# Cross-attention and gated feed-forward: V times the output weights once per head ahead of the rounds, one packed product per round, and the last feed-forward by tiles of 128 rows

## The reference

```python
# x (8, 256, 256), ctx (8, 77, 256); 16 heads of 64; hidden size 768; all fp32
xn   = layernorm(layernorm(x)) * gamma + beta
q    = (xn @ w_q).reshape(B, 256, 16, 64)
k, v = split(ctx @ w_kv)                       # (B, 77, 16, 64) each
attn = softmax(einsum('bqhd,bkhd->bhqk', q * 64 ** -0.5, k))
o    = einsum('bhqk,bkhd->bqhd', attn, v).reshape(B, 256, 1024)
x    = x + (o @ w_out + b_out) * tanh(gate)
y    = layernorm(x)                            # weights below are integers / 127
x    = x + (silu(y @ wg.T) * (y @ wu.T)) @ wd.T
```

## Time and profile before

| | us |
|---|---|
| three runs | 316.48, 316.53, 320.73 |
| median | 316.53 |
| the profiled execution | 315.11 |
| its span in the trace | 313.3 |
| granted TensorE clock, mean | 0.998 |
| T0 of rounds 0 to 7 starts at | 60.4, 90.0, 121.5, 151.0, 180.6, 210.1, 239.7, 269.1 |
| end of O1 of the last round | 293.3 |

### The profile page before, as it was taken

One profiled execution on the slowest core, in us unless ns is written; L12 is line 12 of the kernel. 1 busy time (PEld: TensorE's weight loads), 2 busy tenths in 40 slices (PEclk: granted clock), 3 DMA queues, 4 the chain that ended last, 5 costly groups with the idle time before them and its releaser, 6 DMA issues.

```text
span 313.3 us, 6353 instructions
## 1 busy us (share of the span) xinstructions
PE 295.8 (94%) x2371; PEld 272.2 (87%) x2371; DVE 231.6 (74%) x599; ACT 170.6 (54%) x325; POOL 165.7 (53%) x164
## 2 busy tenths in 40 slices
PE   6899999897987999999999999999999999999994
PEld 6898977686985999889988989898989899978984
DVE  2298887586785887878887787779787878785653
...
DMA packets 16314, 23.29 MB, mean 74 GB/s; under 512 B 1634, under 2 KB 13898, under 8 KB 16282
## 3 DMA queue, kind: packets, MB, share of 16 engines
...
HBM read 15.87 MB, written 4.62 MB: 65 GB/s over the span
## 4 chain that ended last, share of the span: by engine, by line
PE 77%; POOL 11%; DVE 3%; issue 3%; ACT 3%; DMA 2%; POOLq 0%; SPq 0%; DVEq 0%; ACTq 0%
PE ps L786 12%; PE ps L736 8%; PE ps L722 7%; PE ps L696 5%; PE ps L704 5%; PE ps L700 5%; PE ps L623 4%; PE ps L832 4%; PE ps L836 4%; PE ps L833 4%; PE ps L816 3%; PE ps L819 3%; POOL probs L1045 3%; POOL t_lo L1052 3%; PE ps L631 2%
## 5 line engine op out<-in xcount | busy, mean ns | idle before, releaser
L1045 POOL TENSOR_TENSOR probs<-probs,total 128x616 f32<-128x616 f32 x32 | 38.9, 1217 | 75.5 <-DVE total L1170 75.5
L917 ACT COPY pt<-ps 77x512 f32<-77x512 f32 x64 | 34.1, 583 | 49.1 <-PE ps L722 49.1
L1052 POOL TENSOR_TENSOR t_lo<-t_all,t_hi 128x1232 fp32r<-128x1232 f32 x16 | 45.5, 2846 | 4.7 <-ACT t_hi L942 4.7
L1061 POOL TENSOR_TENSOR h_lo<-hid,h_hi 128x256 fp32r<-128x256 f32 x42 | 30.9, 735 | 28.4 <-ACT h_hi L977 28.4
L722 PE MATMUL ps<-ident,probs 128*77 128x128 f32 x256 | 33.4, 273 | 4.0 <-POOL probs L1045 2.9
L832 PE MATMUL ps<-wo_hi,o_hi 128*128 128x256 f32 x128 | 36.4, 284 | 0.0
L833 PE MATMUL ps<-wo_lo,o_hi 128*128 128x256 f32 x128 | 36.1, 282 | 0.0
L836 PE MATMUL ps<-wo_hi,o_lo 128*128 128x256 f32 x128 | 36.0, 281 | 0.0
L1153 DVE TENSOR_REDUCE top<-ps 128x4 f32<-128x308 f32 x64 | 28.7, 472 | 9.1 <-PE ps L704 8.9
L722 PEld LDWEIGHTS ps<-ident,probs 128*77 128x77 f32 x256 | 29.5, 147 | 5.1 <-POOL probs L1045 3.6
L696 PE MATMUL ps<-t_hi,xn_hi 128*128 128x308 f32 x128 | 30.7, 321 | 0.7 <-ACT v_out L876 0.7
...
## 6 DMA issues: line engine op xcount, KB each, us to landing
...
v_scratch<-v_out SPq DMA_DIRECT2D x4, 512.0 KB, 2.9
...
```

What stands on the lines that cost most here:

```text
L917: nc.scalar.copy(pt[:, q * HB:(q + 1) * HB, t * P:(t + 1) * P], ps_p[0:K, m % 2, :].rearrange("k (h q) -> k h q", h=HB)).then_inc(pt_copie ...
L1045: nc.gpsimd.tensor_tensor(p, p, total[:, u, :].unsqueeze(2).to_broadcast([P, HG, K]), ALU.mult).then_inc(probs_done, 1)
L1052: nc.gpsimd.tensor_tensor(t_lo[:, :, cols], t_all[:, :, n, cols], t_hi[:, :, cols].bitcast(F32), ALU.subtract).then_inc(tlo_done, 1)
```

## The change

**V·Wo ahead.** The `v` jobs now make Vᵀ per pair of heads, and 24 new `W` jobs multiply it by the head's 64 rows of w_out: VW[b,h] = V[b,h]·Wo[h], 77×256 per head and batch. `store_vw` writes it to `vw_scratch` in DRAM, cut where a batch ends, into 104 transfers. Stage buffers A to H are reused. Batch 0 of heads 8 to 15 is written straight into `vw_first`.

**The round.** The 8 heads of a group lie packed behind each other (616 rows = 4×128 + 104), so T transposes 128 columns at a time, and U0, U1 transpose the last 104 of both tiles. `values`, `o_hi` and `o_lo` are gone. `project` multiplies packed probabilities (hi and lo) by packed VW (hi and lo): 60 products in place of 48. VW of the next batch is loaded by four transfers per round; VH0, VH1 (ACT), VL0 (DVE) and VL1 (POOL) split it.

**Softmax.** In units 0 and 1 (`BIASED`; 0 to 2 in round 0) DVE no longer subtracts: ACT takes the exponential from PSUM with the negative maximum as its bias, head by head (8 instructions of 128×77 per unit).

**Order.** The transposes of the feed-forward weights (`f` jobs), the casts of w_out and more now lie in the t phase; the t jobs take 3 pairs of banks in turn rather than 4, copied head by head, 11 of 32 jobs by ACT alone, the others one head by ACT and one by DVE. S0 to S3 of round 0 lie between the W jobs. The last feed-forward goes tile by tile (`PE_END`: 128 columns per product, no warm-up there).

```diff
-PE_ORDER = "T0 S2 T1 X1T S3 V0 XT G0 G1 G2 T2 G3 S0 T3 G4 G5 V1 S1 O0 O1 D0 D1".split()
-ACT_ORDER = "Ta C0 C1 E2 X1 O0 X WO t0 t1 E3 t2 h0 C2 Tb t3 h1 C3 h2 t4 E0 h3 O1 h4 t5 h5 E1".split()
-PE_START = "v0 XT v1 v2 v3 S0 v4 FL S1 v5 v6 v7 v8 v9".split()
+BIASED = (0, 1)
+BIASED_FIRST = (0, 1, 2)
+PE_ORDER = "T0 S2 T1 X1T XT S3 G0 G1 G2 U0 S0 G3 G4 T2 S1 T3 G5 U1 O0 O1 D0 D1".split()
+DVE_ORDER = "LN1 LN M2 X1 L0 M3 L1 H0 Z2 H1 Z3 M0 VL0 Q0 H2 L2 H3 L3 H4 Q1 Z0 M1 H5 R0 Z1 R1 AG Y0 Y1".split()
+ACT_ORDER = "VH0 C0 Ta X1 C1 X VH1 t0 E2 t1 h0 E3 Tb t2 K0 h1 t3 E0 C2 h2 t4 C3 h3 t5 K1 h4 E1 h5".split()
+POOL_ORDER = "Ta X VL1 P2 h0 P3 h1 B h2 Tb P0 h3 h4 h5 P1".split()
+PE_START = (
...
+    "W01 W02 v2 IF S0.0 W10 W11 W12 S1.0 W20 W21 v3 W22 v4 S2.0 W30 W31 W32 S3.0 v5 XT.1 W40 W41 W42 W50 v6 "
+    "W51 W52 v7 W60 W62 W70 W61 W71 W72 T0.0 T1.0 S0.1 U0.0 T2.0 T3.0 U1.0 S1.1 O0.0 T0.1 O1.0 XT.2 T1.1 S2.1 "
...
+PE_END = "O0.7 O1.7 xa D0.7 ga0 ga1 ga2 ga3 ga4 ga5 xb D1.7 gb0 gb1 gb2 gb3 gb4 gb5 da db".split()
...
-                if kind == "v":
...
-                        mm(o, ct_hi[:, c, rs], wv_hi[:, c, cols], start=c == 0, stop=False)
...
+                if kind == "W":
...
+                    terms = ((vt_hi, wo_hi), (vt_hi, wo_lo), (vt_lo, wo_hi))
+                    for r in range(2 * p, min(2 * p + 2, RC)):
...
+                            for e in range(2):
+                                ds = slice(e * DH, (e + 1) * DH)
+                                ins = mm(ps[0:m, banks_of(n)[e], at_d:at_d + D], v[ds, i % 2, r * P:r * P + m], w[ds, i, :],
+                                         start=at == 0, stop=at == len(terms) - 1)
...
+            def store_vw(n):
+                _, i, p = jobs[n]
+                evacuated(sp, n)
+                src = stage[slot_of(i, p)]
+                for r in range(2 * p, min(2 * p + 2, RC)):
+                    for b, k, at, count in pieces(r):
...
+                        sp.dma_start(vw_scratch[b, 2 * i:2 * i + 2, k:k + count, :].rearrange("e k d -> k e d"),
+                                     block_rows).then_inc(s_stage[slot_of(i, p)], 16)
...
-            def values(b, g):
-                pe.wait_ge(pt_copied, 8 * b + 4 * g + 4)
...
-                            ins = mm(ps_p[e * DH:(e + 1) * DH, i, pair * Q:(pair + 1) * Q],
-                                     v[:, gh * DH:(gh + 1) * DH], pt[:, h, :], start=True, stop=True)
...
             def project(b, t):
...
-                for i in range(IC):
...
-                    mm(o, o_hi[:, i, ts], wo_hi[:, i, :], start=i == 0, stop=False)
-                    mm(o, o_hi[:, i, ts], wo_lo[:, i, :], start=False, stop=False)
...
-                    ins = mm(o, o_lo[:, i, ts], wo_hi[:, i, :], start=False, stop=i == IC - 1)
+                for g in range(2):
+                    if t == 0:
+                        pe.wait_ge(vwhi_done, 2 * b + g + 1)
+                        pe.wait_ge(pthi_done, 6 * b + 3 * g + 3)
+                    for pt, vw in ((pt_hi, vw_hi), (pt_lo, vw_hi), (pt_hi, vw_lo)):
...
+                        for j in range(GC):
+                            m = chunk(g, j)
+                            ins = mm(o, pt[0:m, g * GC + j, ts], vw[0:m, g * GC + j, :],
...
+            def exponentials(b, u):
...
+                    for h in range(HB):
+                        head = r * HB + h
+                        ins = nc.scalar.activation(probs[:, u, head * K:(head + 1) * K],
+                                                   ps[:, score_bank(half), h * K:(h + 1) * K], ACT.Exp,
+                                                   bias=top[:, u, head:head + 1])
...
+            def gate_up_tile(t, f, general):
...
+                for w, at in ((wg, t * P), (wu, Q + t * P)):
+                    for x2 in (x2_hi, x2_lo):
...
+                            ins = mm(o[:, at:at + P], whole(w[:, c, fs], general), whole(x2[:, c, tile(t)], general),
```

More of the change, by code:

```diff
@@ new lines, in packed, with direct, stores_of @@
+        def packed(h):
+            out, at = [], (h % HG) * K
+            end = at + K
+            while at < end:
+                upto = min((at // P + 1) * P, end)
+                out.append((h // HG * GC + at // P, at % P, at - (h % HG) * K, upto - at))
+                at = upto
+            return out
+        def direct(i, b):
+            return b == 0 and 2 * i >= HG
+        def stores_of(i, p):
+            return sum(sum(len(packed(2 * i + e)) for e in range(2)) if direct(i, piece[0]) else 1
+                       for r in range(2 * p, min(2 * p + 2, RC)) for piece in pieces(r))
@@ new lines, in xattn_ffn_kernel, with free_before, target_of_head @@
+        stored = {}
+        for j in jobs:
+            if j[0] == "W":
+                s = slot_of(*j[1:])
+                stored[j] = 16 * stores_of(*j[1:]) + max([v for k, v in stored.items() if slot_of(*k[1:]) == s], default=0)
+        def free_before(j):
+            same = [k for k in jobs if k[0] == "W" and slot_of(*k[1:]) == slot_of(*j[1:])]
+            at = same.index(j)
+            return stored[same[at - 1]] if at else 0
+        def target_of_head(n, e):
+            j = jobs[n]
+            if j[0] == "W":
+                src = stage[slot_of(*j[1:])]
+                return src[0:rows(RC - 1), e, :] if j[2] == 2 else src[:, e, :, :]
+            head = 2 * j[1] + e
+            return t_half[j[2]][:, :, j[3], head * K:(head + 1) * K]
@@ L1081, in _ @@
             start(POOL_START, stages)
-            first_round(POOL_ORDER, stages)
-            other_rounds(POOL_ORDER, stages)
+            rounds(POOL_ORDER, stages, POOL_START + POOL_END)
+            start(POOL_END, stages)
         @block.vector
@@ L1190, in hidden @@
                 dve.wait_ge(tanh_done, n + 1)
-                if f >= 2 and not last(b):
+                if f >= 2:
                     dve.wait_ge(hlo_done, n - 1)
```

1189 lines of the change are left out of this document (743 added, 446 removed), and 15 rows, old and new, of tables (ACT_START, DVE_START, PE_START).

## The result

| | before | changed |
|---|---|---|
| median, us | 317.19 (4 runs beside it, 316.48 to 320.73) | 368.12 (4 runs, 367.56 to 368.59) |
| ratio | | 1.158, interval 1.149 to 1.167 |
| span of the profiled execution, us | 313.3 | 365.7 |
| T0 of rounds 0, 1, 2, 7 | 60.4, 90.0, 121.5, 269.1 | 113.6, 131.3, 172.6, 322.7 |
| end of O1 of the last round | 293.4 | 345.7 |

The change makes the kernel 16% slower. The forecast was 303 us with a range of 291 to 328: wrong in sign, and the time lies 40 us outside. The span is 64.8 us longer than the sum had it (365.7 against 300.95). By stage, the 52.4 us between the spans are: up to T0 of round 0, +53.2; round 0, −11.9; round 1, +9.8; rounds 2 to 6, +2.6; the last round, −1.3; the end, 0.

A forecast was written before the change was run, and what follows sets the result against it. It took PE, busy 94% of the span, to bound the kernel. From a span of 313.3: +27.6 to T0, −16.4 round 0, −19.3 rounds 1 to 6, −4.6 last round, +0.35 end, plus 1.8 around: 303 us, range 291 to 328.

The forecast's parts named there:

- the sum: Whole span: the profiled span plus the changes of all stages, 300.95 us, before 1.8 around it.
- 49.8 forecast: Start of W: t phase ending at 46.4, then V jobs 0 and 1 taking 3.4 us.
- 88 forecast: T0 of round 0, set by SP's queue up to W job 5,2's stores, landing and a last copy; +27.6 us.
- 0.36 from one to the next: W phase: spacing in us of SP's issues, 81 entries of its queue taking 29 to 41 us.
- my upper bound, 0.50: W phase: dearer spacing of SP's issues, as at the start; worth +8 us, 311 in all.
- PE's 32.3 us of work: W phase: PE's products, V jobs, S0 to S3 and XT, which alone would put T0 at 82.
- 2 us for loads that come late: Round 1: extra loss beyond a steady round, because it is still behind loads.
- PE's sum: Steady rounds: PE's work falls by a net 3.65 us, leaving 25.9 per round.
- None of the three is above PE: Steady rounds: DVE 24.3, ACT 17.6 and POOL 20.2 us stay below PE's 25.9; 0.4 added for DVE's waits.
- Rival B: End: 128-column products run at plain fp32 rate, 0.244 us each, +13 us, 316 us in all; chance 0.11.
- A: W phase: small transfers crowd the first DMA engines, 7.7 us per pair, T0 at 108, 327 us; chance 0.33.
- PE behind stores: W phase: sign for A, with T0 of round 0 at 108.
- C: Rounds: DVE becomes the bound, 27.2 to 27.7 us each, 308 to 311 us in all; chance 0.16.

The follow-up runs named there:

- c2: Changed kernel with whole-block stores, stage buffers in another turn, POOL's `t_lo` behind both `x_hat` pairs, later `TG`, later x loads, new round 1 order: 348.01 us, 1.098.
- c3: c2 without the pieces written straight into `vw_first`, with batch 1's residual loaded earlier and P1.1 ahead of B.1: 345.95 us, 1.091.
- c4: e8 with stage buffers in another turn, `TG` later and, in round 1, copies ahead of the VW splits: 347.11 us, 1.099.
- e9: c3 with stores of 16 rows, packing of 2 rows per head and x loads in place of VW, for time only: 330.26 us, 1.044.
- e4: Changed kernel with five whole-block stores per pair of heads and packing by batch as DRAM to DRAM transfers: 365.13 us, 1.157.
- e8: e6 with POOL scaling probabilities ahead of the residual in rounds 0 and 1, in round 0 also ahead of `XS2`: 344.21 us, 1.088.
- e6: Changed kernel with POOL's `t_lo` also waiting for the next batch's `x1_hat` and `x_hat` pairs: 352.14 us, 1.112.
- e2: Changed kernel with store pieces cut at multiples of 16 rows, VW reaching the wrong heads, for time only: 368.42 us, 1.167.

## Why the prediction was wrong

Of the 64.8 us by which the span is longer than the sum, 25.6 lie ahead of T0 of round 0, 17.5 in rounds 0 and 1, 18.7 in rounds 2 to 6 and 3.3 in the last round; the end gives 0.3 back.

**Up to the first W job, 49.8 forecast, 52.2 measured.** The t phase ended at 48.4 in place of 46.4. ACT was not free from the start: its first token, `TG`, waited for a transfer. ACT in the changed kernel:

```profile
27.89 0.20 ACT L1155 ACTIVATE tgate<-tgate 128x1 f32<-128x1 f32 x1 [2.32 <-DMA bias<-in_L_xattn_b_out]
```

But that is a small part of it: the four kernels with `TG` later (c2, c3, c4, e9) start W at 51.6 to 52.6, the others, with `TG` first, at 52.2 to 53.1. From 28.0 to 46.4 PE is busy for 17.7 us of 18.4 and ACT for 17.0. I had let one of them set the phase; both were near their limit at once. Which of the two terms is short no run divides.

**T0 of round 0, 88 forecast, 113.6 measured: the largest step that failed.** 23 of the 25.6 us lie in the W phase. I named the right place (SP's entries ahead of W job 6's buffers) and the wrong price: "0.36 from one to the next", taken from two loads whose instruction had nothing beside it, and "nearer to 0.36, because those rows too lie in the running kernel". Measured, 0.56, and my upper bound, 0.50, was too low as well. But the price alone is not it, for with fewer issues (e4) T0.0 comes only 4.8 us earlier. What failed is the form of the sum, one queue issuing back to back, one landing (2.9) and one copy behind it, and all engines under it. Measured, `stage_e` makes every pair wait for the landing of the one before (3.6 to 5.6), SP itself waits 6.3 us for copies, and PE loses clock behind its waits. The experiments divide the 25.6: whole blocks, other buffers, dropped pieces, moved statistics and the later `TG` together (c3) 11.4, of which fewer issues with nearly the same order (e4) are 4.8; the bytes on top (c3 to e9) 7.1; and 7.0 are left to 88. Of these, 1.8 are the later start of W; the rest are engines: PE's 32.3 us of work needs 37.0 busy (e9), and PE waits 6.

**Round 0, 13.2 against 17.7, and round 1, 28.3 against 41.3.** I took 2 us for loads that come late. What came late was not the loads alone but POOL, which stood behind them: in round 0, P0.1 behind the residual (5.1 us by e8). In round 1 splits of VW and `x_hat` collide with POOL (in the changed kernel 3.08 for 1.48, and 4.13 for a pair of `x_hat`), PE waits 6.3 us for that pair, and the clock is at half for 10.2 us. The sum had no term for it.

**Steady rounds, 26.3 against 30.8.** PE's sum was right: round 2 took 26.53, and with the collision away they take 27.08, 0.8 over it. The step that failed is "None of the three is above PE". It compared busy times, engine by engine, and asked of each whether it had room. It did not ask what DVE and POOL do to each other when an order puts them side by side. Each loss of 2.7 us on PE brings 1.7 more by the clock, which I had in no term. Over the whole kernel this is 16 us by e6. One meeting is left in e6 as in the changed kernel: in each steady round DVE's `vw_lo` takes 1.7 to 1.9 us for 1.48, and the scaling of probabilities on POOL beside it 2.46 for 1.22. What it costs no run shows.

**Last round and end.** 19.7 against 23.0: PE alone is busy for 20.2 and DVE for 20.5, both above my figure, and PE waits 2.0 once for POOL's probabilities. The end was forecast at +0.35 and came at 0.0 (19.96 against 19.94), though no run has the tiled end alone. Gate and up of one tile, in the chain of the changed kernel:

```profile
347.85 5.32 PE ps L992 x48
```

That is 0.111 a product, against 0.109 forecast, and hardly less than the 0.119 of one with 256 columns: half the width and twice the count nearly doubled PE's time there. Rival B, plain fp32 rate (0.244), is false.

**The rivals.** A had the right sign and near enough the right T0 (108 against 113.6), and the sign that I had set for it, PE behind stores, came. That was luck: landings are shorter with pieces of 16 rows (some 4 to 2.3 us in e2), yet with that the time stayed, and its 327 is 41 short. C, DVE as the bound with maxima late, was not it: DVE is at 87% in the slow rounds, and PE waited for `x_hat`. Its rounds of 27.2 to 27.7 were too short all the same. Two costs were outside of all cases, and the range that was put around them could not hold the time.

**What stays open:** how the 42.0 us of round 1 with hardly any stores (e9) divide between POOL's late work, the statistics that moved, the splits of VW that meet, and the clock; which term of the t phase was short; and what in c4 takes back the gain of its earlier T0.
